# Four layers of convolutions on one core: who issues the transfers that stack three picture rows, where two loads stand in SyncE's order, and four row slots in place of three

## The chip, the cores and the metric

One core of a Trainium2 chip runs the whole program. The metric is the time of one execution on the device in microseconds (us); the time before is the median of three runs. One further execution was recorded by the hardware profiler, and every row quoted below comes from it. Engines: PE is TensorE's matmul, PEld its weight load, DVE is VectorE, ACT is ScalarE, POOL is GpSimd, SP is SyncE. SPq and ACTq are the sequencers of SP and ACT when they issue a transfer (DMA).

## The reference, cut to what matters

The input x has 32 images of 32 channels and 32 x 32 pixels. Four layers follow one another, each added to what it reads (`_gn` normalises every channel of every image on its own):

```
x = x + _L0_conv_ref(_gn(x), ...)   # 8 x 8 patches (10 x 10 windows), best of 8 experts for each patch, 3 x 3 convolution, relu
x = x + _L1_conv_ref(_gn(x), ...)   # one 3 x 3 convolution for each image, its weights a mix of 4 experts
x = x + _L2_conv_ref(_gn(x), ...)   # every pixel replaced by the nearest of 512 codes
x = x + _L3_conv_ref(_gn(x), ...)   # deformable 3 x 3: 9 samples for each pixel, bilinear, at learnt offsets
```

## The kernel before, in words

The 32 images are worked on in eight groups of four; four images of 32 channels fill the 128 partitions. Group g passes through a **front** (`front(g)` in the program of each engine: layers 0, 1 and 2 and the start of layer 3) and then through 32 **tiles** of layer 3 (four images times eight blocks of 128 pixels). A tile is cut into three **thirds** (`third(J)`, tile N = J // 3). For one third PE multiplies tents (the interpolation weights along the rows) by a picture (12 recorded matmuls, L1161), DVE multiplies the result by `near` (L845) and adds up (L852). ACT makes the tents: two `Abs` over a row of `zs` (L629), then one `Relu` (L633), two tiles ahead of PE. A row of `zs` is one tile's sampling rows, broadcast from DRAM to all partitions by SP (`spread_rows`, L319, 576 KB each) into one of SPREADS slots.

The order on every engine is written out by hand. The table PLACE deals the 96 thirds of group g-1 out over the stages of front(g): row0 (8 thirds), row1 (7), row2 (8), row3 (7), y (7), features (1), pool (5), mix (3), conv1 (1), norm2 (3), scores (32), spell (1), pick (1), norm3 (3), rows (3), near (6). It starts 21 thirds early, so that row0, row1 and most of row2 of front(g) hold the last 21 thirds of group g-2's tiles. `at(name, first, end)` plays the thirds of one stage. front(0) has no thirds, and front(1) has its first two at the end of row2. After front(7) the rest of the last group's thirds follow alone.

What SP does in a front, in its order:

- `third(J)`, for the first third of each tile: `spread_rows(N + SPREADS + 1)`. It waits until tent N + 1 is done (`tent_ready`), and for the first row of a group until `z_rows` has been written (`rows_out`). So SP goes through its order at the pace of ACT's tents.
- `load_slice(k, v)`, v = 0 to 4: the windows and expert weights of one fifth of layer 0. Twelve transfers of 50 KB (L394) and one of 720 KB (L396). There are three slots; slice v uses slot v % 3, so slice 3 waits until PE has done convolution 0 and slice 4 until it has done convolution 1. PE's `conv(v)` (L1218) waits for slice v: conv(0) ahead of row0, conv(1) behind row0, conv(2) behind row1, conv(3) behind row2, conv(4) behind row3.
- `y_out_rows`, `y_in_rows`, `windows(k)`: layer 0's result out to DRAM and back, and the next group's windows out.
- `stack_rows(g)` behind the stage features: waits for `xn1_ready` (DVE, L798) and issues six transfers of 136 KB (L374) from `xp1` to `xs1`, those of images 0 and 1. ACT issues the six of images 2 and 3 itself (L681), after its own wait for `xn1_ready`; on ACT `root(g, 1)` (the square root of the norm, L607) stands ahead of that wait, and the thirds of the stage pool behind it. PE's layer-1 convolution (L1245), behind the stage mix, waits for both and for `bd_ready` (DVE, the mixed weights, L997).
- at the end of front(g): slice 0 of the next group, the stages norm3 and rows, `load_picture(g)` (four transfers, L332, after the four of ACT at L742), the first three thirds of near, slices 1 and 2 of the next group, the last three thirds of near.
- for g = 0 alone, the first SPREADS + 1 rows of `zs`.

DVE's `normalise(k)` (the next group's first norm) stands between the fourth and the fifth third of row0. It waits for ACT's `root(k, 0)`, which on ACT stands behind the same four thirds. POOL gathers expert weights, copies windows and adds up the middle third of each tile.

`rowsum` (DVE, L876) and `codes` (L497, L822, L825) are buffers of their own; both are used at other times than `block` and `zs`.

Of the kernel before, what the change touches and what calls it, by code (L numbers as in the profile page):

```python
# [15 lines left out]
B, C, H, W = 32, 32, 32, 32  # L16
PIX = H * W
IMG = 4
GROUPS = B // IMG
P = IMG * C  # L20
PS = 8
NV = H // PS + 1
PATCHES = NV * NV
WIN = PS + 2
G0 = NV * PS + 2
# [5 lines left out]
G1 = W + 2  # L31
# [7 lines left out]
THIRDS = 3  # L39
DENSE = TAPS // THIRDS  # L40
TENTS = 3
SPREADS = 3
SHIFT = 21
ZR = IMG * TAPS
FLATS = 2
# [2 lines left out]
CCH = CODES // 128  # L48
# [8 lines left out]
SLICES = 3  # L57
# [17 lines left out]
def build(nc, A):  # L75
    ctx = ExitStack()
    with ctx:
        def sb(name, shape, dt=F32):
            return ctx.enter_context(nc.sbuf_tensor(name, shape, dt))
# [18 lines left out]
        broute = sb("broute", [128, E1])  # L98
        cb2 = sb("cb2", [128, CODES])
        negone = sb("negone", [C, 1])  # L100
        codes = sb("codes", [128, CCH * C])
        codes_b = sb("codes_b", [128, PARTS, CCH * C], BF16)
        wgrid = sb("wgrid", [128, IMG * 2 * TAPS])
        bgrid = sb("bgrid", [128, 2 * TAPS])
# [20 lines left out]
        wsum = sb("wsum", [128, PATCHES])  # L125
        feat = sb("feat", [ITEMS, C])
        feat_t = sb("feat_t", [C, ITEMS])
        rowsum = sb("rowsum", [128, G0, NV])
        lg = sb("lg", [ITEMS, 6, E0])
        mx = sb("mx", [ITEMS, 4])  # L130
        expert = sb("expert", [ITEMS, 2], U32)
# [5 lines left out]
        xp1 = sb("xp1", [128, G1 * G1])  # L137
# [13 lines left out]
        pos = sb("pos", [128, 2, IMG, TILES * TAPS])  # L151
        near = sb("near", [128, 2, IMG, TILES, TAPS, XW])
        block = sb("block", [128, IMG, TILES, TAPS])
        z = sb("z", [128, TILES, IMG, TAPS])
        zs = sb("zs", [128, SPREADS, TAPS * 128])
        tent = sb("tent", [128, TENTS, KC, TAPS, 128])
        xs1 = arena[0:3 * C, 2560:2560 + IMG * H * G1].rearrange("p (i n) -> p i n", i=IMG)
        picked = [arena[0:ITEMS, 0:PICK],
# [8 lines left out]
        codes_rest = fin[:, CODES:CODES + CCH * C]  # L167
# [48 lines left out]
        xn1_ready = sem("xn1_ready")  # L216
        stacked = [sem(f"stacked{n}") for n in range(2)]
# [31 lines left out]
        rows_out = sem("rows_out")  # L249
        spread_in = [sem(f"spread_in{u}") for u in range(SPREADS)]  # L250
        picture_loaded = [sem(f"picture_loaded{q}") for q in range(XB)]
# [39 lines left out]
        def _(sp):  # L291
# [77 lines left out]

            def stack_rows(g):  # L370
                sp.wait_ge(xn1_ready, g + 1)
                for i in range(2):
                    for dy in range(3):
                        sp.dma_start(xs1[C * dy:C * (dy + 1), i], xp1[C * i:C * (i + 1), G1 * dy:G1 * (dy + H)]  # L374
                                     ).then_inc(stacked[0], 16)

            def load_slice(k, v):
                if v >= SLICES:
# [21 lines left out]
            def front(g):  # L400
                k = g + 1 if g + 1 < GROUPS else None

                def at(name, first=0, end=None):
                    for J in thirds_at(g, name, first, end):
                        third(J)

                full = MOST * C // PATCHES

                def y_out_rows(part, rows, n0, n1):
                    sp.wait_ge(yc_done, NV * g + rows)  # L410
                    if part == 0 and g > 0:
                        sp.wait_ge(y_in, 16 * 2 * IMG * g)
                    for i in range(IMG):
                        sp.dma_start(y_dram[i].rearrange("(p c) s -> c p s", c=C)[:, n0:n1],
                                     yc[C * i:C * (i + 1), PS * PS * n0:PS * PS * n1].rearrange(
                                         "c (p s) -> c p s", s=PS * PS)).then_inc(y_out[i], 16)

                def y_in_rows(part, c0, c1):
                    for i in range(IMG):
                        sp.wait_ge(y_out[i], 16 * (2 * g + part + 1))  # L420
                        sp.dma_start(yb[C * i + c0:C * i + c1, :],
                                     y_dram[i].rearrange("(c n) s -> c (n s)", c=C)[c0:c1]).then_inc(y_in, 16)

                for v in range(NV - 1):
                    at(f"row{v}")
                    if v + SLICES < NV:
                        load_slice(g, v + SLICES)
                    if v == 2 and k:
                        features_out(k)
                y_out_rows(0, NV - 1, 0, MOST)  # L430
                if k:
                    features_in(k)
                y_in_rows(0, 0, full)
                y_out_rows(1, NV, MOST, PATCHES)
                at("y", 0, 3)
                y_in_rows(1, full, C)
                at("y", 3)
                if k:
                    windows(k)
                at("features")  # L440
                stack_rows(g)
                at("pool")
                at("mix")
                at("conv1")
                at("norm2")
                for t in range(TILES):
                    at("scores", 4 * t, 4 * t + 4)
                    if t == 2 and k:
                        store_weights(k, 0)
                    if t == 6 and k:  # L450
                        store_weights(k, 1)
                at("spell")
                at("pick")
                if k:
                    load_slice(k, 0)
                at("norm3")
                at("rows")
                load_picture(g)
                at("near", 0, 3)
                if k:  # L460
                    load_slice(k, 1)
                    load_slice(k, 2)
                at("near", 3)
                if g == 0:
                    for N in range(SPREADS + 1):
                        spread_rows(N)
# [18 lines left out]
        def _(pool):  # L485
# [5 lines left out]
            for i in range(IMG):  # L491
# [2 lines left out]
            pool.dma_start(wmix[:], A["w_mix"]).then_inc(loaded_later, 16)  # L494
            pool.dma_start(broute[:], A["b_route"].partition_broadcast(128)).then_inc(loaded_later, 16)
            pool.dma_start(cb2[0:C, :], A["codebook_t"]).then_inc(loaded_later, 16)
            pool.dma_start(codes[:].rearrange("p (k c) -> p k c", c=C),  # L497
                           A["codebook"].rearrange("(k p) c -> p k c", p=128)).then_inc(loaded_later, 16)
            pool.dma_start(bgrid[:], A["b_grid"].partition_broadcast(128)).then_inc(loaded_later, 16)
            for r in range(3):  # L500
# [66 lines left out]
            for g in range(GROUPS):  # L567
                k = g + 1 if g + 1 < GROUPS else None
# [30 lines left out]
        def _(act):  # L599
# [60 lines left out]
            def front(g):  # L660
                k = g + 1 if g + 1 < GROUPS else None
# [13 lines left out]
                at("y")  # L675
                at("features")
                root(g, 1)
                act.wait_ge(xn1_ready, g + 1)
                for i in range(2, IMG):
                    for dy in range(3):  # L680
                        act.dma_start(xs1[C * dy:C * (dy + 1), i], xp1[C * i:C * (i + 1), G1 * dy:G1 * (dy + H)]  # L681
                                      ).then_inc(stacked[1], 16)
                at("pool", 0, 2)
                act.wait_ge(z_ready, g + 1)
                act.activation(sm1[:, 2], sm1[:, 1], ACT.Exp, scale=-1.0).then_inc(ez_ready, 1)
# [87 lines left out]
        def _(dve):  # L773
# [34 lines left out]
            def prepare():  # L808
                for t in (xp1[:], xs2[:], cb2[C:2 * C, :], cb2[2 * C:, :]):
                    dve.memset(t, 0.0)  # L810
                dve.drain()
                dve.memset(xs2[C:C + 1, :, :], 1.0)
                dve.memset(negone[:], -1.0)
                dve.wait_ge(loaded_later, LOADS_LATER)
                dve.memset(ones_h[:], 1.0)
                dve.tensor_copy(ident_h[:], ident[:])
                g = grid[:].rearrange("p a (t k) -> p a t k", k=TAPS)
                bias = bgrid[:].rearrange("p (k a) -> p a k", a=2).unsqueeze(2)
                dve.tensor_tensor(g, g, bias.broadcast_to([128, 2, TILES, TAPS]), ALU.add)

                for k in range(PARTS):
                    dve.tensor_copy(codes_b[:, k, :], codes[:] if k == 0 else codes_rest)  # L822
                    dve.drain()
                    if k < PARTS - 1:
                        dve.tensor_tensor(codes_rest, codes[:] if k == 0 else codes_rest, codes_b[:, k, :],  # L825
                                          ALU.subtract)
                        dve.drain()

                dve.tensor_tensor(cbsq, cb2[0:C, :], cb2[0:C, :], ALU.mult).then_inc(sq_ready, 1)
                dve.wait_ge(norms_ready, 1)  # L830
                dve.tensor_copy(cb2[C:C + 1, :], P5[C:C + 1, :])
                dve.tensor_scalar(cb2[0:C, :], cb2[0:C, :], 2.0, None, ALU.mult)
# [40 lines left out]
            def features(k):  # L873
                dve.drain()
                a = xp0[:]
                dve.tensor_reduce(rowsum[:], bass.AP(a.tensor, a.offset, [a.ap[0], [G0, G0], [PS, NV], [1, WIN]]),  # L876
                                  AX.X, ALU.add)
                dve.drain()
                a = rowsum[:]
                dve.tensor_reduce(wsum[:].rearrange("p (v h) -> p v h", h=NV),  # L880
                                  bass.AP(a.tensor, a.offset, [a.ap[0], [PS * NV, NV], [1, NV], [NV, WIN]]),
                                  AX.X, ALU.add)
                dve.drain()
                dve.tensor_scalar(wsum[:], wsum[:], 1.0 / (WIN * WIN), None, ALU.mult).then_inc(wsum_ready, 1)
# [514 lines left out]
```

## Time and profile before

| | |
|---|---|
| runs | 2309.24, 2313.58, 2314.66 us |
| median | 2313.58 us |
| profiled execution: its own time | 2312.38 us |
| its span | 2310.6 us (1.8 us lie around it) |
| PE busy | 1936.0 us (84%) |
| DVE busy | 1610.2 us (70%) |
| ACT busy | 1512.9 us (65%) |
| mean granted TensorE clock | 0.944 |
| bytes moved by transfers | 323.99 MB |

PE is busy 84% of the span. The other engines are below that, and all wait for one another by turns, so what matters is the stretches in which PE waits. The fronts of groups 1 to 7 look alike and follow one another every 268 us or so.

### The profile page before, as it was taken

To read this page: it belongs to the slowest core of one execution; us is meant where nothing else is said; L and a number is where in the kernel's file an instruction comes from. 1 tells how busy PE (TensorE), PEld (TensorE's weight loads), DVE (VectorE), ACT (ScalarE), POOL (GpSimd) and SP (SyncE) were. 2 spreads that over 40 slices of the span, in tenths; PEclk is the share of its full clock that TensorE was granted. 3 is DMA by queue.
4 is the path that set the end of the run, shared out by engine and by line. 5 is a ranking of instruction groups with operands and counts; after the bars stand their busy time and mean duration, and the time that the engine had idled before them with its cause. 6 is when DMAs were issued, how large, how long until landed. Compare 5 with 4: busy or idle time off the path is not lost.

```text
span 2310.6 us, 52567 instructions
## 1 busy us (share of the span) xinstructions
PE 1936.0 (84%) x20746; PEld 1688.0 (73%) x20746; DVE 1610.2 (70%) x3285; ACT 1512.9 (65%) x1787; POOL 479.6 (21%) x858
## 2 busy tenths in 40 slices
PE   0346479989799889998799897998899997999999
PEld 0212377779678777888677796788777886879998
DVE  2158368966698558985689566985589756986665
ACT  0012367768586767767576685867577585869986
POOL 2000121132111221131211321122211311114222
PEclk9968699999999899999999899999999999999999
DMA  6743754566445763566545664547534663223331
GB/s 187 145 124 92 163 160 136 144 158 163 131 148 144 178 169 104 163 143 165 156 134 157 162 165 121 150 146 186 158 114 149 152 176 109 73 76 125 111 117 58
DMA packets 258759, 323.99 MB, mean 140 GB/s; under 512 B 201268, under 2 KB 212244, under 8 KB 254292
## 3 DMA queue, kind: packets, MB, share of 16 engines
q1 hardware_dynamic: 240644, 274.52, 43.0%
q0 software_dynamic: 3280, 29.86, 5.1%
q10 hardware_dynamic: 14592, 16.26, 2.7%
q8 instruction: 166, 2.72, 0.5%
q14 instruction: 77, 0.63, 0.1%
HBM read 251.21 MB, written 55.99 MB: 133 GB/s over the span
## 4 chain that ended last, share of the span: by engine, by line
PE 55%; DVE 15%; DMA 7%; DVEq 7%; SPq 6%; issue 4%; ACT 3%; ACTq 3%; POOL 0%; POOLq 0%
PE bank L1161 39%; PE bank L1259 7%; SPq L394 6%; PE bank L1148 3%; DVEq L1029 2%; PE bank L1218 2%; DMA zs<-z_rows 2%; DVE samp L852 2%; DVE code L1030 2%; DVEq L851 2%; DVE onehot L1037 2%; PE bank L1136 2%; ACTq L681 1%; PE bank L1278 1%; DVE strip L845 1%
## 5 line engine op out<-in xcount | busy, mean ns | idle before, releaser
L1161 PEld LDWEIGHTS bank<-picture,tent 128*128 128x128 f32 x9216 | 1317.0, 194 | 183.1 <-issue 106.3
L1161 PE MATMUL bank<-picture,tent 128*128 128x160 f32 x9216 | 1378.2, 305 | 49.5 <-DVE strip L845 47.1
L845 DVE TENSOR_TENSOR strip<-bank,near 128x480 f32<-128x480 f32 x768 | 498.5, 652 | 305.3 <-PE bank L1161 299.0
L629 ACT ACTIVATE tent<-zs,row_at_sb 128x1152 f32<-128x1152 f32 x512 | 624.5, 1250 | 101.5 <-DMA zs<-z_rows 89.7
L633 ACT ACTIVATE tent<-tent 128x2304 f32<-128x2304 f32 x256 | 544.1, 2125 | 20.7 <-issue 2.0
L555 POOL TENSOR_TENSOR strip<-strip 128x192 f32<-128x192 f32 x256 | 137.9, 539 | 1531.2 <-DVE strip L845 1531.2
L852 DVE TENSOR_REDUCE samp<-strip 128x96 f32<-128x480 f32 x512 | 334.4, 653 | 47.8 <-issue 1.3
L1259 PE MATMUL bank<-cb,xs 128*128 128x512 f32 x512 | 273.2, 616 | 16.4 <-ACT xs L698 8.5
L1148 PE MATMUL bank<-ident_sb,samp 128*96 128x128 f32 x768 | 128.8, 278 | 86.1 <-ACT fin L614 72.7
L1028 DVE MAX8 top<-bank 128x8 f32<-128x512 f32 x256 | 176.9, 691 | 30.9 <-PE bank L1259 30.6
L1030 DVE FIND_INDEX8 code<-top,bank 128x8 uint32<-128x512 f32 x256 | 176.8, 691 | 0.3 <-issue 0.3
L618 ACT COPY samp_t<-bank 96x384 f32<-96x384 f32 x256 | 118.7, 464 | 86.6 <-PE bank L1148 66.1
L698 ACT COPY xs<-xn 32x128 f32<-32x128 f32 x256 | 75.7, 296 | 144.6 <-PE bank L1259 127.0
L1148 PEld LDWEIGHTS bank<-ident_sb,samp 128*96 128x96 f32 x768 | 91.7, 128 | 92.9 <-issue 88.7
L607 ACT ACTIVATE sd<-ve 128x1 f32<-128x1 f32 x32 | 6.4, 200 | 222.3 <-DVE ve L787 222.3
L557 POOL TENSOR_TENSOR strip<-strip 128x96 f32<-128x96 f32 x256 | 123.1, 481 | 20.1
L705 ACT ACTIVATE diag<-ident_h,code_f 128x128 f16<-128x128 f16 x256 | 81.1, 387 | 55.2 <-DVE code_f L1055 55.2
L1259 PEld LDWEIGHTS bank<-cb,xs 128*128 128x128 f32 x512 | 81.5, 190 | 48.5 <-issue 33.4
L561 POOL TENSOR_TENSOR samp<-strip 128x96 f32<-128x96 f32 x256 | 107.4, 419 | 36.9 <-POOL strip L557 0.4
L939 DVE TENSOR_TENSOR yc<-bank,gb 128x320 f32<-128x320 f32 x40 | 19.7, 491 | 106.7 <-PE bank L1218 106.7
L1037 DVE TENSOR_SCALAR onehot<-spelt,code_at_sb 128x512 bf16<-128x512 f16 x256 | 84.4, 392 | 4.1 <-ACT spelt L712 4.1
L1218 PE MATMUL bank<-slice 96*32 96x64 f32 x1920 | 36.2, 242 | 60.5 <-DMA slice<-picked_weights 59.9
(127 smaller groups left out, 1121.5 us busy)
## 6 DMA issues: line engine op xcount, KB each, us to landing
zs<-z_rows SPq DMA_DIRECT2D x256, 576.0 KB, 4.2
picked_weights<-arena SPq DMA_DIRECT2D x15, 1800.0 KB
arena<-picked_weights SPq DMA_DIRECT2D x24, 720.0 KB, 7.2
arena<-windows SPq DMA_DIRECT2D x288, 50.0 KB, 2.7
slice<-picked_weights SPq DMA_DIRECT2D x16, 720.0 KB, 6.2
windows<-arena SPq DMA_DIRECT2D x32, 312.5 KB, 5.4
slice<-windows SPq DMA_DIRECT2D x192, 50.0 KB, 2.3
arena<-xp SPq DMA_DIRECT2D x48, 136.0 KB, 4.9
```

The source lines that it names most:

```text
L394: sp.dma_start(xs0[s][C * dy:C * (dy + 1), i], a[:, :, dy * WIN:dy * WIN + CUT]).then_inc(sliced[s], 16)
L555: pool.tensor_tensor(y[:, :, 0:2], y[:, :, 0:2], y[:, :, 2:4], ALU.add).then_inc(summing, 1)
L629: act.activation(w[:, piece], zs[:, N % SPREADS, :], ACT.Abs, bias=row_at[:, piece:piece + 1])
L633: act.activation(w, w, ACT.Relu, bias=1.0, scale=-1.0).then_inc(tent_ready, 1)
L845: dve.tensor_tensor(y, STRIPS[J % 3][:, 0:DENSE * XW * C].rearrange("p (d c x) -> p d c x", d=DENSE, c=C), w.broadcast_to([128, DENSE, C, ...
L852: m = dve.tensor_reduce(samp[:, N % 2, PARTK * d:PARTK * (d + 1)], strip[:, d], AX.X, ALU.add)
L1028: dve.max(top[:, i, :], SCORES[n % 2][:, :])
L1030: dve.max_index(code[:, i, :], top[:, i, :], SCORES[n % 2][:, :]).then_inc(score_read, 1)
L1037: m = dve.tensor_scalar(onehot[:, c, :], spelt[:], code_at[:, c:c + 1], None, ALU.is_equal)
L1148: m = pe.transpose(PT[0:PARTK, 128 * r:128 * (r + 1)], samp[:, N % 2, PARTK * r:PARTK * (r + 1)], ident[:])
L1161: m = pe.matmul(STRIPS[j % 3][:, XW * C * e:XW * C * (e + 1)], tent[:, N % TENTS, c, DENSE * d + e], picture[:, b % 2, i, c], start=(c == ...
L1259: pe.matmul(SCORES[n % 2][:, :], xs2[:, i, :], cb2[:], start=True, stop=True).then_inc(score_done, 1)
```

## The change: what it does

1. SP issues all twelve stacking transfers; ACT issues none and no longer waits for `xn1_ready`. The two counts of `stacked` stay: images 0 and 1, images 2 and 3.
2. At the end of a front `load_picture(g)` moves behind the first three thirds of near; slice 1 of the next group moves behind the last three.
3. Slice 2 moves out of the end of a front into the next one, between the fourth and the fifth third of row0.
4. SPREADS goes from 3 to 4: rows of `zs` are fetched one tile further ahead.
5. `rowsum` lies in the place of `block`, and `codes` in slot 0 of `zs`.

```diff
-SPREADS = 3
+SPREADS = 4
...
-        codes = sb("codes", [128, CCH * C])
...
-        rowsum = sb("rowsum", [128, G0, NV])
...
         block = sb("block", [128, IMG, TILES, TAPS])
+        rowsum = block[:].rearrange("p i t d -> p (i t d)")[:, 0:G0 * NV].rearrange("p (h v) -> p h v", h=G0)
         z = sb("z", [128, TILES, IMG, TAPS])
         zs = sb("zs", [128, SPREADS, TAPS * 128])
+        codes = zs[:, 0, 0:CCH * C]
...
             def stack_rows(g):
                 sp.wait_ge(xn1_ready, g + 1)
-                for i in range(2):
+                for i in range(IMG):
                     for dy in range(3):
                         sp.dma_start(xs1[C * dy:C * (dy + 1), i], xp1[C * i:C * (i + 1), G1 * dy:G1 * (dy + H)]
-                                     ).then_inc(stacked[0], 16)
+                                     ).then_inc(stacked[i // 2], 16)
...
-                for v in range(NV - 1):
+                at("row0", 0, 4)
+                if g > 0:
+                    load_slice(g, 2)
+                at("row0", 4)
+                load_slice(g, SLICES)
+                for v in range(1, NV - 1):
                     at(f"row{v}")
                     if v + SLICES < NV:
                         load_slice(g, v + SLICES)
...
                 at("norm3")
                 at("rows")
+                at("near", 0, 3)
                 load_picture(g)
-                at("near", 0, 3)
+                at("near", 3)
                 if k:
                     load_slice(k, 1)
-                    load_slice(k, 2)
-                at("near", 3)
                 if g == 0:
                     for N in range(SPREADS + 1):
                         spread_rows(N)
...
                 root(g, 1)
-                act.wait_ge(xn1_ready, g + 1)
-                for i in range(2, IMG):
-                    for dy in range(3):
-                        act.dma_start(xs1[C * dy:C * (dy + 1), i], xp1[C * i:C * (i + 1), G1 * dy:G1 * (dy + H)]
-                                      ).then_inc(stacked[1], 16)
                 at("pool", 0, 2)
```

## Rows read from the trace of the kernel before

**Rows 1.** The page, chain that ended last, shares by line

```profile
PE bank L1161 39%; PE bank L1259 7%; SPq L394 6%; PE bank L1148 3%; DVEq L1029 2%; PE bank L1218 2%; DMA zs<-z_rows 2%; DVE samp L852 2%; DVE code L1030 2%; DVEq L851 2%; DVE onehot L1037 2%; PE bank L1136 2%; ACTq L681 1%; PE bank L1278 1%; DVE strip L845 1%
```

**Rows 2.** Waits, whole span: engine, line, releaser: total us, times, longest

```profile
ACT tent L629 <- DMA zs<-z_rows: 89.7, 7, 20.5
...
PE bank L1148 <- ACT fin L614: 72.7, 8, 10.5
...
PE bank L1161 <- DVE strip L845: 47.1, 5, 10.4
```

**Rows 3.** Timeline of SP, end of front(2): start, us taken, [idle, releaser]

```profile
749.79 0.34 SPq L319 DMA_DIRECT2D zs<-z_rows  x1
754.16 5.58 SPq L394 DMA_DIRECT2D arena<-windows  x12
...
760.39 10.69 SPq L394 DMA_DIRECT2D arena<-windows  x12
...
771.60 12.54 SPq L319 DMA_DIRECT2D zs<-z_rows  x4
```

**Rows 4.** Timeline of ACT, DVE and PE in the same stretch

```profile
763.92 2.12 ACT L633 ACTIVATE tent<-tent 128x2304 f32<-128x2304 f32 x1
...
765.50 5.05 PE L1161 MATMUL bank<-picture,tent 128*128 128x160 f32 x36
...
770.28 0.15 DVE L787 TENSOR_SCALAR ve<-mv 128x1 f32<-128x1 f32 x1
...
779.11 1.25 ACT L629 ACTIVATE tent<-zs,row_at_sb 128x1152 f32<-128x1152 f32 x1 [12.70 <-DMA zs<-z_rows]
...
782.93 3.57 PE L1161 MATMUL bank<-picture,tent 128*128 128x160 f32 x12 [10.41 <-DVE strip L845]
...
786.42 2.89 PE L1218 MATMUL bank<-arena 96*32 96x64 f32 x120
```

**Rows 5.** Timeline of PE, the same place in front(7)

```profile
1854.30 0.85 PE L1148 MATMUL bank<-ident_sb,samp 128*96 128x128 f32 x3 [4.89 <-ACT samp_t L618]
1854.94 6.05 PE L1161 MATMUL bank<-picture,tent 128*128 128x160 f32 x36
```

**Rows 6.** Timeline around the stacking transfers of front(3)

```profile
855.89 0.20 ACT L607 ACTIVATE sd<-ve 128x1 f32<-128x1 f32 x1 [6.63 <-DVE ve L787]
...
857.97 4.30 SPq L374 DMA_DIRECT2D arena<-xp  x6
857.98 4.41 ACTq L681 DMA_DIRECT2D arena<-xp  x6
862.48 0.27 ACT L614 COPY fin<-bank 128x128 f32<-128x128 f32 x1 [6.39 <-issue]
...
863.53 6.80 PE L1161 MATMUL bank<-picture,tent 128*128 128x160 f32 x36
...
879.84 2.78 PE L1245 MATMUL bank<-arena,mix 96*32 96x512 f32 x24 [0.86 <-DVE mix L997]
```

**Rows 7.** Issue to landing: line L374 (SP), then L681 (ACT), 48 each

```profile
DMA to landing us min/median/max: 2.5/4.9/6.0
...
DMA to landing us min/median/max: 2.6/4.9/6.1
```

**Rows 8.** Timeline, first group: stacking, layer-1 convolution, slice 3 and its conv(3)

```profile
129.66 4.46 SPq L374 DMA_DIRECT2D arena<-xp  x6
...
140.13 8.69 PE L1245 MATMUL bank<-arena,mix 96*32 96x512 f32 x48 [8.21 <-DVE mix L997]
...
270.17 5.70 SPq L394 DMA_DIRECT2D slice<-windows  x12
...
282.21 3.43 PE L1218 MATMUL bank<-slice 96*32 96x64 f32 x120 [7.23 <-DMA slice<-picked_weights]
```

**Rows 9.** Windows: us, busy (x count) of PE PEld DVE ACT POOL, PEclk, DMA share, GB/s

```profile
740.00:780.00 40.00, 32.51 (x368) 31.58 (x366) 22.73 (x43) 22.74 (x23) 14.15 (x16) 0.94 0.75 184
...
845.00:852.00 7.00, 7.00 (x71) 6.56 (x70) 5.10 (x10) 4.01 (x4) 2.57 (x6) 1.00 0.96 272
```

More of the change, by code:

```diff
@@ L496, in _ @@
             pool.dma_start(cb2[0:C, :], A["codebook_t"]).then_inc(loaded_later, 16)
-            pool.dma_start(codes[:].rearrange("p (k c) -> p k c", c=C),
+            pool.dma_start(codes.rearrange("p (k c) -> p k c", c=C),
                            A["codebook"].rearrange("(k p) c -> p k c", p=128)).then_inc(loaded_later, 16)
@@ L821, in prepare @@
                 for k in range(PARTS):
-                    dve.tensor_copy(codes_b[:, k, :], codes[:] if k == 0 else codes_rest)
+                    dve.tensor_copy(codes_b[:, k, :], codes if k == 0 else codes_rest)
                     dve.drain()
                     if k < PARTS - 1:
-                        dve.tensor_tensor(codes_rest, codes[:] if k == 0 else codes_rest, codes_b[:, k, :],
+                        dve.tensor_tensor(codes_rest, codes if k == 0 else codes_rest, codes_b[:, k, :],
                                           ALU.subtract)
@@ L875, in features @@
                 a = xp0[:]
-                dve.tensor_reduce(rowsum[:], bass.AP(a.tensor, a.offset, [a.ap[0], [G0, G0], [PS, NV], [1, WIN]]),
+                dve.tensor_reduce(rowsum, bass.AP(a.tensor, a.offset, [a.ap[0], [G0, G0], [PS, NV], [1, WIN]]),
                                   AX.X, ALU.add)
                 dve.drain()
-                a = rowsum[:]
+                a = rowsum
                 dve.tensor_reduce(wsum[:].rearrange("p (v h) -> p v h", h=NV),
```

## The prediction, made before the change was run

> **What bounds the kernel now.** I read the chain that ended last first. It is mostly PE at the tiles of layer 3, as a kernel with PE busy 84% should show, but two lines in it are no work at all: 6% is SP issuing slices (L394) and 1% is ACT issuing stacking transfers (L681) [rows 1]. Next I read the waits, which say whom this holds up. ACT stands seven times, 89.7 us in all, for a row of `zs`; PE stands five times, 47.1 us, for DVE's L845, and seven times of about 10 us (the eighth is under 1) for ACT's L614 [rows 2]. Then the timelines around one of each show how the waits are built.
>
> *Stall A, at row0.* SP issues the row of tile 27 at 749.79, then waits for `z_rows`, issues slice 1 from 754.16 and slice 2 from 760.39; the next row of `zs` (tile 28) leaves only at 771.60 [rows 3]. ACT had finished tent 27 at 766.04 and starts tent 28 at 779.11, 12.7 us idle. DVE had its variance ready at 770.28+0.15, but the root it waits for stands behind tent 28 on ACT. PE runs out of read banks and stands 10.4 us [rows 4]. Slice 2, which blocked the queue, is not used until conv(2), behind row1. This happens at the start of fronts 2 to 6. In front(7) there is no next norm, and PE stands 4.9 us [rows 5].
>
> *Stall B, at pool.* ACT has the root done at 856.09. It then waits for xn1, spends 4.4 us on six issues, and only at 862.48 copies the result that PE's L1148 waits for. This is in fronts 1 to 7 [rows 6].
>
> **The change part by part.**
>
> *Slice 2 out of the end of the front, picture and slice 1 later, fourth slot (stall A).* I walk SP's new order on the old times. The row of tile 28 is now the one that leaves at 749.8, in the place of tile 27's. The four picture transfers follow; they are some 4 us later than now and first read at tile 28 of the previous group's work, over 35 us on: nothing. SP was released by tent 24 at 749.8 and tent 27 is done at 766.04 [rows 3, 4], so tents are 5.4 us apart: 25 at 755.2, 26 at 760.6. With tent 25 row 29 leaves. Slice 1 then goes out from about 755.9 to 762 (12 issues in 5.58 us and one more [rows 3]), 2 us later than now. Landing may take as long as the 7.5 us from 771.60 to 779.11 that a row of `zs` took in this traffic [rows 3, 4]: 769.5. PE stood from 772.5; without that it would do one more third and want conv(1) at about 775: hidden, 5 us of cover. Were the cover gone, it would cost what exceeds 5 us. Row 30 leaves at 762, row 31 when tent 27 is done (766.0 [rows 4]), slice 2 from 766.5 to 772.5. Slice 2 lands by 780, and conv(2), seven thirds behind conv(1), wants it near 789: hidden, cover 10 us. Row 32 leaves at about 774 with tent 28, and ACT wants it near 788. Slice 3 is issued 10 us earlier than now. So ACT's wait goes. What is late next is DVE's own norm: ACT's root could follow only at 779.11 + 1.25 = 780.4, and PE started 2.6 us later [rows 4]; with the root at 770.6 the bank is free at 773.2, and PE would come to it at 772.5. About 0.75 us of wait stays.
>
> For fronts 2 to 6: 47.1 - 5 x 0.75 = 43.4 us. The clock comes on top. After such a stall 12 matmuls take 3.57 us, against 5.05 / 3 = 1.68 at full clock, and conv(1) 2.89 us where half of the fully cold 3.43 us is 1.7 [rows 4, 8]. The first is 1.9 each; of the second, up to 1.2, I take half, 0.6: 5 x 2.5 = 12.5. Front(7): 4.9 + (6.05 - 5.05) = 5.9 [rows 4, 5]. **Stall A gives 61.8 us.** The same 4-slot depth changes nothing elsewhere, since ACT waits for `zs` only these seven times [rows 2].
>
> *All stacking transfers on SP (stall B).* ACT's copy moves from 862.48 to just behind the root, 856.09: 6.4 us, and PE with it, x 7 = 44.7 us. PE still stands 3.8 us, for the variance comes from DVE. The clock: 36 matmuls took 6.80 instead of 5.05 us [rows 4, 6]. The idle time of 4.9 us in front(7) cost 1.0 [rows 5]; I keep that 1.0 and take back 0.75 x 7 = 5.2. **Stall B gives 49.9 us**, if the twelve transfers land in time. SP needs 12 x 0.72 = 8.6 us from 857.97, until 866.6; with 4.9 us to landing [rows 7] that is 871.5. PE's convolution would be ready at 879.84 - 6.4 - 0.75 = 872.7 [rows 6]. That is 1.2 us of cover, the thinnest in this sum; with the longest landing, 6.0, it is gone exactly. Behind `stack_rows` on SP stand rows of `zs` that ACT wants three tiles on: 4.3 us more don't reach them.
>
> Here a rule speaks about the change. The rows first: six issues hold ACT 4.4 us, about as long as one transfer takes to land, 4.9 [rows 6, 7], and PE pays for it. The Trainium skill (DMA: Bandwidth & Descriptors, "Issuing engines are not separate DMA queues") says that issuing from several engines saves only the sequencers' time, usually small against the transfer. By that rule the second half of the issue time would be worth little either way, and the sum would lack stall B, 50 us. I go by the rows.
>
> *First group.* front(0) has no thirds to hide under. SP's twelve issues from 129.66 at 0.74 us end at 138.6; landing after 2.5 to 4.9 us [rows 7, 8] gives 141.1 to 143.5, where PE was ready at 140.13. **Cost 2.2** (bounds 0 to 3.4). At front(1) slice 2 now stands behind five rows of `zs`, the fifth of which waits for tent 0. Slice 2's thirteen issues, some 7 us, now follow those rows instead of standing ahead of them, so slice 3 is issued at about 270 as before, and slice 2 from about 263. Slice 3 had landed 12 us after its first issue [rows 8]; so does slice 2, I take: conv(2) at 275, 3.4 us of it, then two thirds of up to 3.57 us, then conv(3) at 285 or a little before, in place of 282.2. **Cost 3** (bounds: a gain of 4 if landing is as quick as in the fronts, a loss of 9).
>
> *`rowsum` and `codes` in other places.* No instruction, size or wait is added: 0.
>
> **Sum**: 61.8 + 49.9 - 2.2 - 3 = 106.5 us, from 2312.4 to 2205.9. The median stood 1.2 us above the profiled execution: **2207 us**. All bytes stay; nothing else on PE's path moves.
>
> **Rivals.**
>
> *Stacking lands late (0.11).* The landing of the last transfers is behind the cover of 1.2 us by 2 to 4 us in each front, since twelve transfers now go through one queue right behind four of 312 KB. For it: the cover is thin. Against it: SP's and ACT's six landed equally fast [rows 7]. 7 x 3 = 21 us: 2228. A rule leads to the same place: the Trainium skill (same page, "Queues, rings and completion order") says that each transfer engine takes turns between SP's row of rings and ACT's. By it ACT's six would get past SP's backlog now and no longer after; rows 7 show no such advantage.
>
> *Transfers bound, not issue (0.08).* The near stretch moves 184 GB/s at a share of 0.75 [rows 9]; if this is all the queue gives for such small pieces, rows of `zs` stay late, and half of stall A stays: 2207 + 31 = 2238. Against it: 272 GB/s at 0.96 a little later [rows 9].
>
> *Slower (0.03).* Slice 1 stands behind the last thirds of near, so behind one more wait for a tent and one more row of `zs`. If SP gets there late, conv(1) stands and all thirds behind it. It begins to cost when slice 1 lands 5 us later than I place it, and makes the kernel slower from 5 + 106.5 / 6 = 23 us on. At 25 us: 2207 + 6 x 20 = 2327.
>
> *No effect (0.02).* The root and the copy wait for something that the trace doesn't name, and both stalls stay: 2312.
>
> Forecast (0.76): its own range 2190 to 2222. Below it lies only that PE's 3.8 us at stall B costs no clock (7 us) and the first group costs nothing (4 us). **Range** 2186 to 2244, to take in the first two rivals. What this kernel's measurement can tell from no change is 0.3%, 7 us. Faster by more: 0.95; within: 0.02; slower: 0.03.
>
> **What would show it.** ACT's wait for `zs` in the table of waits falls from 89.7 to under 25 us (what stays is the first one, of 20.5, at group 1), PE's wait for L845 from 47.1 to some 5, and PE's for L614 from 72.7 to about 28, with L614 starting some 0.2 us after L607. L394 leaves the chain but for the start. The mean clock rises. PE's L1245 shows no wait for a transfer beyond the first group. The forecast is wrong if L1245 or L1218 wait for transfers in each front, or if ACT shows a new wait between L607 and L633.

## The result and the profile after

The changed kernel takes **2211.78 us** (median of 4 runs, 2209.31 to 2213.41), against 2312.33 us for the kernel before in the same runs: a ratio of 0.9565, 95% interval 0.9548 to 0.9582. That is 100.6 us less. The forecast was 2207, range 2186 to 2244. The profiled execution took 2213.27 us, its span is 2211.5.

The page of the changed kernel: span, busy time of PE, DVE and ACT, and the chain that ended last by line (L1160 is what was L1161: line numbers behind the edit of SP's order have moved by +4, those behind the issues taken from ACT by -1).

```profile
span 2211.5 us, 52567 instructions
...
PE 1932.0 (87%) x20746; PEld 1680.2 (76%) x20746; DVE 1607.2 (73%) x3285; ACT 1512.8 (68%) x1787; POOL 482.9 (22%) x858
...
PE bank L1160 47%; PE bank L1258 7%; PE bank L1147 3%; PE bank L1217 3%; DVEq L1028 2%; DVE samp L851 2%; DVE code L1029 2%; DVEq L850 2%; PE bank L1135 2%; SPq L394 2%; DVE onehot L1036 2%; DVE strip L844 2%; DVE stats L777 1%; PE bank L1277 1%; DMA tent<-in_Wexp,expert 1%
```

PE, DVE and ACT are busy as long as before, to within 4 us; it is their waits that fell. SP's issues (L394) fell from 6% of the chain to 2%, and ACT's issues of stacking transfers are gone from it [rows 1]. L394 is in the chain only up to 271 us, in the first two fronts, and the mean granted clock rose from 0.944 to 0.959. Waits of the changed kernel, whole span (engine, line, releaser, total us, times, longest); they answer to [rows 2]:

```profile
ACT tent L633 <- DMA zs<-z_rows: 11.1, 1, 11.1
...
PE bank L1147 <- ACT fin L618: 26.4, 7, 4.0
```

ACT waits once for a row of `zs`, at group 1, in place of seven times and 89.7 us. PE's wait for ACT's copy went from 72.7 to 26.4 us. The third wait of [rows 2], 47.1 us, is now a part of this group (busy us, mean ns, idle before, releasers), 3.5 us:

```profile
L1160 PE MATMUL bank<-picture,tent 128*128 128x160 f32 x9216 | 1371.4, 304 | 5.0 <-DVE strip L844 3.5 <-issue 1.4
```

The timeline of SP, DVE and PE at stall A, the front that answers to [rows 3, 4] (times from the span's start):

```profile
731.51 0.34 SPq L319 DMA_DIRECT2D zs<-z_rows  x1
732.02 7.22 SPq L394 DMA_DIRECT2D arena<-windows  x12
739.28 0.49 SPq L396 DMA_DIRECT2D arena<-picked_weights  x1
739.81 2.80 SPq L319 DMA_DIRECT2D zs<-z_rows  x2
742.79 6.83 SPq L394 DMA_DIRECT2D arena<-windows  x12
...
746.92 0.16 DVE L789 RECIPROCAL nr<-sd 128x1 f32<-128x1 f32 x1 [0.27 <-ACT sd L611]
...
749.36 1.90 PE L1160 MATMUL bank<-picture,tent 128*128 128x160 f32 x12 [0.64 <-DVE strip L844]
751.18 1.88 PE L1217 MATMUL bank<-arena 96*32 96x64 f32 x120
```

Between two slices SP now issues rows of `zs`. DVE waits 0.27 us for its root, PE stands 0.64 us (the forecast left 0.75), and conv(1) takes 1.88 us where it took 2.89. Before, DVE's wait at this place was:

```profile
780.49 0.16 DVE L790 RECIPROCAL nr<-sd 128x1 f32<-128x1 f32 x1 [10.05 <-ACT sd L607]
```

The same at stall B, with the layer-1 convolution behind it ([rows 6]):

```profile
820.16 0.50 PE L1147 MATMUL bank<-ident_sb,samp 128*96 128x128 f32 x3 [3.69 <-ACT fin L618]
820.50 5.06 PE L1160 MATMUL bank<-picture,tent 128*128 128x160 f32 x36
...
835.07 2.78 PE L1244 MATMUL bank<-arena,mix 96*32 96x512 f32 x24 [0.87 <-DVE mix L996]
```

PE stands 3.69 us (forecast 3.8), and the convolution waits for the mixed weights, not for a transfer. Only in the first group does it wait for one (7.6 us, below). The median time from issue to landing is shorter than the 4.9 us of [rows 7], but this is for each transfer by itself; the twelve together are no quicker, as stack_only shows. L374, the changed kernel, 96 transfers:

```profile
DMA to landing us min/median/max: 2.3/2.6/4.1
```

### The profile page after: what moved, and what is told of

Read it like the earlier page. It is cut to its first block, busy times and chain, and to the rows that moved or that the text cites. A ratio compares the mean times of both kernels' runs of the same rounds, so it can differ in the third digit from the quotient of the medians.

```text
span 2211.5 us, 52567 instructions
## 1 busy us (share of the span) xinstructions
PE 1932.0 (87%) x20746; PEld 1680.2 (76%) x20746; DVE 1607.2 (73%) x3285; ACT 1512.8 (68%) x1787; POOL 482.9 (22%) x858
## 4 chain that ended last, share of the span: by engine, by line
PE 66%; DVE 15%; DVEq 7%; DMA 4%; issue 3%; SPq 2%; ACT 2%; ACTq 0%; POOL 0%; POOLq 0%
PE bank L1160 47%; PE bank L1258 7%; PE bank L1147 3%; PE bank L1217 3%; DVEq L1028 2%; DVE samp L851 2%; DVE code L1029 2%; DVEq L850 2%; PE bank L1135 2%; SPq L394 2%; DVE onehot L1036 2%; DVE strip L844 2%; DVE stats L777 1%; PE bank L1277 1%; DMA tent<-in_Wexp,expert 1%
## 5 line engine op out<-in xcount | busy, mean ns | idle before, releaser
L1160 PEld LDWEIGHTS bank<-picture,tent 128*128 128x128 f32 x9216 | 1310.9, 193 | 140.8 <-issue 110.3
L1160 PE MATMUL bank<-picture,tent 128*128 128x160 f32 x9216 | 1371.4, 304 | 5.0 <-DVE strip L844 3.5
L1258 PE MATMUL bank<-cb,xs 128*128 128x512 f32 x512 | 279.8, 630 | 14.7 <-ACT xs L697 7.7
L1147 PE MATMUL bank<-ident_sb,samp 128*96 128x128 f32 x768 | 127.3, 275 | 35.1 <-ACT fin L618 26.4
L1217 PE MATMUL bank<-arena 96*32 96x64 f32 x2880 | 53.0, 238 | 39.9 <-DMA arena<-picked_weights 38.5
```

The source lines that it names most:

```text
L1147: m = pe.transpose(PT[0:PARTK, 128 * r:128 * (r + 1)], samp[:, N % 2, PARTK * r:PARTK * (r + 1)], ident[:])
L1160: m = pe.matmul(STRIPS[j % 3][:, XW * C * e:XW * C * (e + 1)], tent[:, N % TENTS, c, DENSE * d + e], picture[:, b % 2, i, c], start=(c == ...
L1258: pe.matmul(SCORES[n % 2][:, :], xs2[:, i, :], cb2[:], start=True, stop=True).then_inc(score_done, 1)
```

## The experiments

Ten kernels. Those of one batch shared runs of the kernel before; a difference to the kernel before is to its median in the same batch (2310.51, 2310.62 and 2308.89 us). The changed kernel was run in a batch of its own, so a difference to it carries both intervals, some 7 us.

### Which part of stall A's cure does the work?

**slot_only.** The kernel before with the fourth slot and the two shared buffers, nothing moved.

```diff
-SPREADS = 3
+SPREADS = 4
```

> The kernel before with the fourth row slot alone (and the two shared buffers that go with it). Theory: stall A is row 28 standing behind slices 1 and 2 on SP; with one more slot row 28 leaves near 749.8 in the old times, and it is row 29 that stands behind the slices, landing at 779 where ACT wants it at 775. ACT then waits some 4 us instead of 12.7, but behind DVE's norm and not ahead of it, and PE hardly notices: stall A gives nearly all of its 62 us, 2250 to 2262. Rival 1, the order of the loads is what counts and the slot adds nothing: 2300 or more. Rival 2, both are needed, half each: about 2280.

2264.56 us, -46.0, ratio 0.9792 (0.9767 to 0.9817); 2.6 us above the expected range.

**order_only.** The three loads moved as in the change, three slots, stacking shared.

```diff
-                for v in range(NV - 1):
+                at("row0", 0, 4)
+                if g > 0:
+                    load_slice(g, 2)
+                at("row0", 4)
+                load_slice(g, SLICES)
+                for v in range(1, NV - 1):
...
-                load_picture(g)
                 at("near", 0, 3)
+                load_picture(g)
+                at("near", 3)
                 if k:
                     load_slice(k, 1)
-                    load_slice(k, 2)
-                at("near", 3)
```

> The kernel before with the loads moved (picture, slice 1, slice 2) and three row slots as before; the stacking is shared by SP and ACT. Theory: row 28 leaves behind tent 25 at about 755.2 in the old times, 11 us ahead of its use, so this alone gives nearly all of stall A too: 2250 to 2265, with at most a few us left at row 32, which leaves behind slice 3. Rival 1, the slot is what counts: 2300 or more. Rival 2, half each: about 2280.

2264.06 us, -46.5, ratio 0.9793 (0.9771 to 0.9815).

**slice2_only.** Only the first half of that diff, and `load_slice(k, 2)` taken out.

> The kernel before with slice 2 alone moved into row0; picture and slice 1 stay, three slots. Theory: row 28 leaves behind slice 1 at about 760.6 in the old times and lands by 765 to 768, ACT wants it at 766.4: ACT waits 0 to 2 us, stall A is all but gone: 2250 to 2268. Rival, the two transfers that went behind the near thirds carry it: slice 2 alone leaves half, 2280.

2262.24 us, -48.3, ratio 0.9793 (0.977 to 0.9816).

**loads_only.** The changed kernel with the stacking shared again: all moves and the slot.

```diff
                 root(g, 1)
+                act.wait_ge(xn1_ready, g + 1)
+                for i in range(2, IMG):
+                    for dy in range(3):
+                        act.dma_start(xs1[...], xp1[...]).then_inc(stacked[1], 16)
...
```

> The changed kernel with the stacking shared by SP and ACT again: the loads moved and the fourth slot, both. Theory: each of the three remedies alone (slot, slice 2, whole order) took 46 to 48 us, so they mend the same wait; together they give little more, at most the 10 to 20 us in all that ACT still waited for rows behind the norm, of which PE saw almost nothing: 2255 to 2264. Rival: the remedies add up, 2240 or less. With stack_only's 45 us this run also says whether stalls A and B are independent: then before minus this plus 45 is the whole 98 us.

2259.82 us, -50.8, ratio 0.9785 (0.9756 to 0.9813).

All four are the same within their intervals, and all stay under the 61.8 us that the forecast gave to stall A (58.8 with the loss it took off for slice 2 at the start). The waits of ACT for rows of `zs`, in slot_only, order_only and slice2_only:

```profile
ACT tent L629 <- DMA zs<-z_rows: 43.0, 7, 20.2
```

```profile
ACT tent L633 <- DMA zs<-z_rows: 13.7, 5, 11.2
```

```profile
ACT tent L633 <- DMA zs<-z_rows: 33.5, 8, 11.9
```

With the slot alone ACT still waits, (43.0 - 20.2) / 6 = 3.8 us a front, as expected behind the norm, and PE pays nothing for it. So the theory holds: one row stood behind 26 issues, and either the fourth slot or slice 2 moved away gets it out in time. The change carries both cures; the second bought nothing that could be measured here. The moves of the picture and of slice 1 were not run by themselves; order_only, which has them, is no faster than slice2_only, which has not.

### Stacking: issue or wait?

**stack_only.** The kernel before with all twelve transfers on SP.

```diff
-                for i in range(2):
+                for i in range(IMG):
...
-                                     ).then_inc(stacked[0], 16)
+                                     ).then_inc(stacked[i // 2], 16)
...
-                act.wait_ge(xn1_ready, g + 1)
-                for i in range(2, IMG):
-                    for dy in range(3):
-                        act.dma_start(xs1[...], xp1[...]).then_inc(stacked[1], 16)
```

> The kernel before with all stacking transfers on SP and nothing else. Theory: PE's stall at L614 falls from 10.2 to 3.8 us in seven fronts, and a little of the clock comes back: 44.7 to 50 us less, 2262 to 2268, stall A unchanged. Rival, stall A has swallowed part of it (the two overlap) or part of the time comes back at PE's L1245: 2275 to 2290. Side question: the twelve transfers, issued by SP alone, land in a median of 2.6 us in the changed kernel and in 4.9 before; if two issuing queues side by side made them slow, it is 2.6 here too; if the traffic around did it, 4.9.

2265.87 us, -44.6, ratio 0.9817 (0.9781 to 0.9853). The landing, with nothing else changed, has a median of 2.6 us where two queues have 4.9, so the traffic around is not what made the difference:

```profile
DMA to landing us min/median/max: 2.4/2.6/3.6
```

That does not make the twelve together quicker. The last transfers in front(3), first of the kernel before (ACT's; the first of the twelve left at 857.97), then of stack_only (the first left at 838.25):

```profile
L681 ACTq DMA_DIRECT2D arena<-xp x2: 786/808/830, 860.7 to 861.6; - x2
...
DMA to landing us min/median/max: 5.9/5.9/5.9
```

```profile
L374 SPq DMA_DIRECT2D arena<-xp x2: 590/598/606, 844.6 to 845.2; - x2
...
DMA to landing us min/median/max: 2.6/2.7/2.7
```

The last one lands 861.6 + 5.9 - 857.97 = 9.5 us after the first issue with two queues, and 845.2 + 2.7 - 838.25 = 9.7 us with one. Over all eight groups it is 9.4 to 9.6 us with two and 9.7 to 10.6 with one. Two queues hand over the twelve in 4.4 us, one in 7.5, and the transfers end at nearly the same time: those handed over sooner take longer each.

The stalls are independent within the intervals: 50.8 + 44.6 = 95.4 of the 100.6 us.

**wait_left.** The changed kernel; ACT waits as before but issues nothing.

```diff
                 root(g, 1)
+                act.wait_ge(xn1_ready, g + 1)
                 at("pool", 0, 2)
```

> The changed kernel, but ACT still waits for xn1_ready in the old place and issues nothing. Theory: stall B was 1.9 us of waiting and 4.4 us of issuing; only the wait comes back, 7 x 1.9 = 13 us: 2221 to 2229. Rival, the transfers' own traffic or their landing made the stall and the place of the wait is nothing: 2212. Rival, the wait alone made it: 2255.

2231.59 us, ratio to before 0.9659 (0.9632 to 0.9686), where the changed kernel had 0.9565: 22 us slower, with an uncertainty of 7, and 2.6 us above the expected range. PE's wait for the copy:

```profile
PE bank L1148 <- ACT fin L618: 40.3, 7, 6.0
```

That is 13.9 us more than the 26.4 above, the 7 x 1.9 us of the wait. The split of stall B, 1.9 us of waiting to 4.4 us of issuing, holds in the trace; the rest of the 22 us, at the edge of the intervals, stays unexplained.

### What is left of PE's waits?

**root_behind.** The changed kernel, ACT's root behind one third.

```diff
+                at("pool", 0, 1)
                 root(g, 1)
-                at("pool", 0, 2)
+                at("pool", 1, 2)
```

> The changed kernel with ACT's root(g, 1) behind the first third of the stage pool and no longer ahead of it. Theory: what is left of stall B, 3.7 us in seven fronts, is ACT waiting for DVE's variance with PE's copy behind it; the copy would be ready some 5 us earlier, so all 26 us go: 2180 to 2190. Rival, DVE is next: its block of residual and norm holds PE's banks whatever ACT does, and only some 1 us of each goes: 2203 or more.

2185.09 us, ratio to before 0.946 (0.9431 to 0.9488), 26.7 us under the changed kernel. As expected: DVE does not hold PE there, ACT's order did; PE's 26.4 us of waiting for the copy are gone from the table of waits.

**relu_ahead.** The changed kernel, a Relu ahead of the next root.

```diff
+                at("norm2", 0, 1)
                 root(g, 2)
                 act.wait_ge(xn2_ready, g + 1)
...
-                at("norm2")
+                at("norm2", 1)
```

> The changed kernel with the first third of the stage norm2 ahead of ACT's root(g, 2). Theory: PE stands 2.6 to 2.9 us at L1135 in seven fronts for a copy of ACT that is behind a Relu of 2.1 us, and ACT idles 3 us ahead of that root; the Relu goes into that idle time, 7 x 2.1 = 15 us: 2195 to 2200. Rival, the root is late then, and with it xn2 and the scores: 2212 or slower.

2189.24 us, ratio 0.9482 (0.9452 to 0.9511): 22.5 us under the changed kernel, where 12 to 17 were expected. PE's wait at this place (L1135, L1136 here) fell from 27.1 to 11.4 us.

**relu_before.** The same move on the kernel before.

> The kernel before with the first third of norm2 ahead of ACT's root(g, 2), nothing else. On the changed kernel this move took 22.5 us where the removed Relu explains 15. Theory: the other 7 are half-clock spells at norm2 (some 32 us of PE's busy time in the changed kernel, which costs 16), and the kernel before has none there; so here the move takes only the 15: 2296 to 2299. Rival, the 22 us are the move's own, whatever the clock did: 2288 to 2291.

2287.13 us, -21.8, ratio 0.991 (0.9892 to 0.9928). My theory of the 7 us fell here and the rival was right: the move takes about 22 us in either kernel. What I had overlooked is that the kernel before also had half-clock spells to lose, if elsewhere (table below): PE's busy time at half clock fell from 77.5 to 52.8 us, most of it at the stage pick (23.9 to 3.4). Half of that and the 15.4 us that left PE's wait (26.8 to 11.4) would be 27.8 us; why it is only 21.8 is open.

**both_ahead.** The changed kernel with both moves.

> The changed kernel with both moves on ACT: the root of layer 1 behind the first third of pool, and the first third of norm2 ahead of the root of layer 2. Theory: the two stalls lie apart and are independent but for the clock; 26 and 22 us alone, so 2160 to 2170 together. Rival, the clock is shared (each has already brought back the same spells): 2170 to 2180.

2157.27 us, ratio 0.9352 (0.9334 to 0.937): 54.5 us under the changed kernel, and 2.7 us below the expected range. The two parts gave 26.7 + 22.5 = 49.2 alone. The 5 us between lie within the intervals, so all that is shown is that the two moves add up; the rival, by which they share the clock's gain, is out by 13 us. Its page:

```profile
span 2154.5 us, 52567 instructions
...
PE 1910.0 (89%) x20746; PEld 1658.7 (77%) x20746; DVE 1606.9 (75%) x3285; ACT 1513.6 (70%) x1787; POOL 481.3 (22%) x858
```

PE is busy 22 us less than in the changed kernel for the same matmuls. Its busy time at half clock fell from 69.2 to 13.7 us, half of the difference is 27.8, so the clock accounts for all of it.

## Why the prediction was right, and which terms were not

**Stalls, right.** The idle time taken from PE was put at 43.4 + 4.9 + 44.7 = 93.0 us. The traces give 52.0 - 3.5 for stall A and 72.7 - 26.4 for stall B: 94.8 us. The experiments show the causes as stated: slices ahead of one row of `zs`; ACT's issues and its wait. Taken by themselves the two cures give less than their terms: 50.8 us (43 to 56, loads_only) for 61.8 - 3 at stall A, and 44.6 (34 to 51, stack_only) for 49.9 - 2.2 at stall B. The second is within its interval; the first is too large, and the next term says by what in part.

**The clock, wrong by 14 us.** The forecast took back 12.5 + 1.0 at stall A and 5.2 at stall B. I read the windows of every stretch between 300 us and the last tiles in which the granted clock was 0.50, and added up PE's busy time in them; half of such time is what the clock costs.

| stage | before | after | changed by (half) |
|---|---|---|---|
| row0 (stall A) | 27.4 | 0 | -13.7 |
| pool (stall B) | 26.3 | 26.7 | +0.2 |
| norm2 | 0 | 32.2 | +16.1 |
| pick | 23.9 | 10.2 | -6.8 |
| all | 77.5 | 69.2 | -4.2 |

The term at stall A is what left that stage (13.7 for 13.5). What failed is the step "The clock comes on top", 18.7 us in all, which took each stall's half-clock time as gone for good: it was gone there and came back at norm2. In loads_only, without the cure of stall B, the half-clock time fell from 77.5 to 59.9 us, a gain of 8.8 and not 13.5. At norm2 PE stands 2.6 to 3.0 us before and after alike (L1136, then L1135). The 7 us around PE's restart there, in fronts 1 and 2, in the kernel before and then in the changed one (us, busy of PE PEld DVE ACT POOL, clock, DMA share, GB/s):

```profile
359.00:366.00 7.00, 6.41 (x57) 5.20 (x58) 4.13 (x9) 6.87 (x10) 2.42 (x4) 1.00 0.57 163
626.00:633.00 7.00, 6.68 (x57) 5.30 (x58) 4.40 (x9) 6.87 (x9) 2.14 (x4) 1.00 0.60 184
```

```profile
347.00:354.00 7.00, 6.18 (x37) 4.68 (x38) 1.47 (x3) 5.62 (x7) 2.38 (x4) 0.52 0.56 163
600.00:607.00 7.00, 6.36 (x39) 4.87 (x40) 1.47 (x3) 5.46 (x7) 2.46 (x4) 0.52 0.55 163
```

At a granted clock of 0.52, nearly all of the stretch at 1.2 GHz, PE does 37 matmuls where it did 57 at 2.4 GHz. The idle time ahead is about the same (2.63 and 2.92 us in front 1). What differs is what PE did before it, 10 us of idle some 30 us earlier in the one and 3.7 in the other, and when the gap fell, which no run controlled. Why one such gap costs the clock and another not is open. At stall B the forecast of 5.2 us had no ground: a gap of 3.7 us cost the clock as much as one of 10 us had, in six fronts of seven.

**The start, wrong by 9 us the other way.** I forecast a loss of 2.2 + 3 us. The first layer-1 convolution (the timeline was cut at 140 us, the convolution goes on):

```profile
127.83 1.22 DVE L976 TENSOR_REDUCE sm<-xp 128x1 f32<-128x1024 f32 x1
...
131.99 3.15 DVE L996 SCALAR_TENSOR_TENSOR mix<-wmix,sm,mix 96x96 f32<-96x96 f32 x12
...
137.65 2.79 PE L1244 MATMUL bank<-arena,mix 96*32 96x512 f32 x12 [7.62 <-DMA arena<-xp]
```

From xn1 it starts after 137.65 - 127.8 = 9.9 us; before it was 140.13 - 129.66 = 10.5 [rows 8]. The transfers are now what it waits for, as forecast, but the mixed weights had been late themselves: ACT's exponential stood behind ACT's six issues, so DVE ended the mix at 140.1 and ends it now at 135.1. I had costed the issues for SP and not for what they held up on ACT. At group 1, conv(2) did come late, at 269.99 (I had said 275), but slice 3 had landed by the time PE wanted it. SP, the kernel before, then the changed one:

```profile
255.66 14.46 SPq L319 DMA_DIRECT2D zs<-z_rows  x4
```

```profile
245.79 12.39 SPq L319 DMA_DIRECT2D zs<-z_rows  x5
...
264.46 6.36 SPq L394 DMA_DIRECT2D slice<-windows  x12
```

I had put slice 3's issues at 270 as before, as if only slice 2 moved. But the rows of `zs` that stood behind slice 2 left 10 us earlier, tent 0 with them, and slice 3 at 264.46. This is also why ACT's first wait, which I had left at 20.5 us, fell to 11.1. PE in the changed kernel:

```profile
269.99 3.43 PE L1217 MATMUL bank<-arena 96*32 96x64 f32 x120 [14.61 <-DMA arena<-picked_weights]
273.34 4.63 PE L1160 MATMUL bank<-picture,tent 128*128 128x160 f32 x24
278.12 1.88 PE L1217 MATMUL bank<-slice 96*32 96x64 f32 x120
```

conv(3) ends at 278.12 + 1.88 = 280.0, where it ended at 282.21 + 3.43 = 285.6 [rows 8]: 5.6 us earlier where I had it 3 us later. 1.9 us of this is that the changed kernel's execution was ahead at xn1 already (127.8 against 129.66), which the change does not explain; 3.8 us are the start's gain.

**Cover of the stacking, right in sign and too thin.** I gave the twelve transfers 1.2 us of cover: 8.6 us of issuing and 4.9 of landing, 13.5 in all. They took about 10 (9.7 to 10.3). Each transfer's 4.9 us of [rows 7] must have held time in which it waited for the others issued in the same 4.4 us; that is argued from the two last landings above. The last one landed near 580 in a front whose convolution starts at 585.00. The rivals "stacking lands late", "transfers bound", "slower" and "no effect" show nothing in the trace. The rule of the Trainium skill (DMA: Bandwidth & Descriptors, "Issuing engines are not separate DMA queues"), by which several issuers save only the sequencers' time, usually small, would have cost the sum its second half: stack_only gives 44.6 us for it. The trace agrees that only the issuing was saved, since the last transfer lands within 0.2 us of the same time in front(3). But the issuing was not small here, 4.4 us of ACT in each front. The other rule (same page, "Queues, rings and completion order"), by which a second queue gets past the first one's backlog, led to the rival that lands late; with one queue the last transfer landed 0.1 to 1.2 us later, and in the changed kernel PE never waited for it after the first group.

**In sum**, the total owes its fit to luck: two errors cancelled. The forecast was 106.5 us; 94.8 + 4.2 + 3.8 at the start = 102.8 from the traces, and 1.9 us of lead at xn1, against 99.1 between the two spans. The other 5.6 us, lost somewhere in small pieces, I can't place.

## What to carry to other kernels

SP goes through its issues in the order of the program, and that turns a load that nobody needs yet into a wait for the one behind it: look for the engine that idles, go back along the issuing queue, and ask which issue could stand later. One cure is enough; the fourth slot alone, or one slice moved alone, did what both did. An issue or a wait also stops the compute behind it on that engine, so count what stands there on every engine it is moved to or from. And don't count the clock with the stall: the idle time came off PE within 2% of the forecast, but much of the half-clock time moved to another gap until the small gaps went too. Nor does the median landing time of one transfer tell when a set of them is there: read when the last one lands.

## What the runs showed that was not expected

- Two queues (SP and ACT) issuing the same twelve transfers of 136 KB side by side show a median of 4.9 us from issue to landing, one queue issuing all twelve 2.6 us (stack_only, no other edit). Yet the last one lands 9.4 to 9.6 us after the first issue in the one, 9.7 to 10.6 in the other.
- Idle gaps of 2.6 to 3.0 us at norm2 cost the clock in six of seven fronts of the changed kernel and in none of the kernel before. Gaps of 2.1 us ahead of L1278 (L1277 in the changed kernel), at the stage pick, were followed by half clock in seven fronts before and three after. Cutting the gaps at norm2 short and removing the 3.7 us ones left PE 13.7 us of busy time at half clock (both_ahead), from 69.2.
- Seven of the ten kernels (all but slice2_only, stack_only and relu_before) show one halt of 3.0 to 3.6 us in the middle of a convolution's 120 matmuls, between 996 and 1048 us, with no releaser named by the profile; order_only:

```profile
1042.63 1.81 PE L1222 MATMUL bank<-arena 96*32 96x64 f32 x113
1047.75 0.32 PE L1222 MATMUL bank<-arena 96*32 96x64 f32 x7 [3.31 <-issue]
```

What PE waits for there is open.
